# Linear attention: two of four q products inside the layer norm, weighting by pairs of tiles, and a projection that begins per tile

## The reference

```python
Q = relu(proj(Wq, bq)); K = relu(proj(Wk, bk)); V = proj(Wv, bv)
decay = exp(-pos / n)[None, None, :, None]
Q = Q * decay
K = K * decay
KV = einsum('bhnd,bhne->bhde', K, V)
Ksum = K.sum(axis=2)
Z = 1.0 / (einsum('bhnd,bhd->bhn', Q, Ksum)[..., None] + EPS)
out = einsum('bhnd,bhde->bhne', Q, KV) * Z
return einsum('bnm,dm->bnd', out, Wo) + bo
```

## Time and profile before

| | |
|---|---|
| runs | 2073.14, 2076.76, 2078.67 us (median 2076.76) |
| profiled execution, its own time | 2071.96 us |
| its span, first to last instruction | 2069.9 us |
| busy: TensorE / VectorE / ScalarE / GpSimd | 88% / 54% / 37% / 27% of the span |
| mean granted TensorE clock | 0.928 |

### The profile page before, as it was taken

One profiled execution on the slowest core, in us unless ns is written; L12 is line 12 of the kernel. 1 busy time (PEld: TensorE's weight loads), 2 busy tenths in 40 slices (PEclk: granted clock), 3 DMA queues, 4 the chain that ended last, 5 costly groups with the idle time before them and its releaser, 6 DMA issues.

```text
span 2069.9 us, 32796 instructions
## 1 busy us (share of the span) xinstructions
PE 1826.2 (88%) x10672; PEld 1016.8 (49%) x10673; DVE 1124.2 (54%) x2329; ACT 757.5 (37%) x1469; POOL 554.8 (27%) x950
## 2 busy tenths in 40 slices
PE   7799999998789996868999697899777999988895
PEld 4344444443456664565666456565443444355553
DVE  6688888884422224762222447532356888665323
ACT  3277777776311111121111112122033667731210
POOL 2322222221211112531111311464032222224630
PEclk9699999998789997978999799999886999999998
DMA  3311111123300003010000221123123112011241
GB/s 108 91 32 39 38 37 40 41 54 151 124 18 25 20 25 99 1 43 18 25 20 25 91 92 43 52 86 124 41 63 72 30 31 40 2 44 61 84 135 41
DMA packets 82064, 114.22 MB, mean 55 GB/s; under 512 B 17273, under 2 KB 61465, under 8 KB 81177
## 3 DMA queue, kind: packets, MB, share of 16 engines
q1 hardware_dynamic: 70808, 82.23, 14.0%
q0 software_dynamic: 11136, 30.42, 4.6%
HBM read 78.35 MB, written 33.69 MB: 54 GB/s over the span
## 4 chain that ended last, share of the span: by engine, by line
PE 70%; DVE 18%; issue 4%; DMA 3%; POOL 1%; ACT 1%; SPq 0%; POOLq 0%; DVEq 0%; ACTq 0%
PE psum L1521 13%; PE psum L1051 8%; PE psum L1035 7%; DVE region_a L799 7%; PE psum L1542 6%; PE psum L996 6%; PE psum L1757 5%; PE psum L1731 3%; PE psum L1775 2%; DVE x_res L1427 2%; PE psum L1776 2%; PE psum L1531 2%; PE psum L1742 2%; DVE ln_stats L269 1%; PE psum L925 1%
## 5 line engine op out<-in xcount | busy, mean ns | idle before, releaser
L799 DVE TENSOR_REDUCE region_a<-psum 128x1 f32<-128x640 f32 (+7 forms) x576 | 528.2, 954 | 108.7 <-PE psum L1001 57.5
L903 ACT ACTIVATE region_w<-psum 128x512 f32<-128x512 f32 x864 | 465.6, 600 | 221.3 <-PE psum L1035 217.8
L1521 PE MATMUL psum<-region_w,region_a 128*128 x608 | 271.1, 599 | 1.5 <-DVE region_a L1602 1.2
L1051 PE MATMUL psum<-region_w,region_a 128*32 128x512 f32 (+3 forms) x2304 | 254.1, 515 | 1.0 <-POOL region_w L726 0.6
L726 POOL TENSOR_SCALAR_AFFINE_SELECT region_w<-region_w 128x512 f32<-128x512 f32 x192 | 122.3, 637 | 457.1 <-ACT region_w L903 452.9
L996 PE MATMUL psum<-region_a,y_norm 48*128 48x512 bf16 (+7 forms) x816 | 224.4, 351 | 4.9 <-DVE region_a L799 4.0
L1416 POOL DMA_INDIRECT answer_rows<-region_a x116 | 114.7, 989 | 420.1 <-ACT region_a L1571 345.6
L1035 PE MATMUL psum<-y_norm,region_a 51*128 51x512 bf16 (+1 forms) x612 | 205.5, 399 | 5.5 <-DMA y_norm<-region_a 3.7
L1521 PEld LDWEIGHTS psum<-region_w,region_a 128*128 128x128 f32 x608 | 113.9, 193 | 132.1 <-issue 132.1
L1609 DVE TENSOR_TENSOR region_a<-psum,region_a 128x512 f32<-128x512 f32 x76 | 52.6, 692 | 215.1 <-PE psum L1521 215.1
L1412 POOL DMA_INDIRECT region_a<-token_rows,region_a x116 | 113.1, 975 | 146.6 <-DVE region_a L1388 86.8
(11 more groups left out here) (218 smaller groups left out, 2636.3 us busy)
## 6 DMA issues: line engine op xcount, KB each, us to landing
y_norm<-a_q SPq DMA_DIRECT2D x132, 64.0 KB
token_rows<-y_norm SPq DMA_DIRECT2D x16, 512.0 KB, 5.2
y_norm<-answer_rows SPq DMA_DIRECT2D x16, 512.0 KB, 6.3
y_norm<-b_q SPq DMA_DIRECT2D x36, 128.0 KB
region_w<-in_f_wg SPq DMA_DIRECT2D x1, 4096.0 KB, 13.4
region_w<-in_f_wu SPq DMA_DIRECT2D x1, 4096.0 KB, 13.5
region_w<-in_f_wd SPq DMA_DIRECT2D x1, 4096.0 KB, 14.9
region_w<-answer_rows SPq DMA_DIRECT2D x8, 512.0 KB, 8.4
```

The costliest lines, as they stand in the source:

```text
L799: dve.tensor_reduce(dst, src, AX_X, ALU.max, negate=True).then_inc(self.ring_done.sem, 1)
L903: act.activation(self.p[col % P_RING][:, :, i % 4, :], c.bank[ST_BANKS[s % 3]].rearrange("p (h t) -> p h t", h=GQ), ACT.Exp, scale=self.sc ...
L1051: mm = pe.matmul(c.bank[ACC_BANK][32 * h:32 * h + 32, P * lo:512], self.vp[slot][:, j, :], self.p[col % P_RING][:, h, lo:4, :], start=(j = ...
L1521: mm = pe.matmul(bank[:, :], self.yt[:, f, :], w[:, f, bass.ds(own * self.hidden + 512 * half, 512)], start=(f == 0), stop=(f == FT - 1))
```

## The change

1. `LayerNorm` gets hooks. Ahead of the transposes of group 2, TensorE does the q product of group 0, and ahead of those of group 3 that of group 1; ScalarE does the two relus behind its copies of groups 1 and 2. `LinearAttention.tensor` does the q products of groups 2 and 3 alone. The routing's own early products go through the same hook at the place that they had.
2. The weighting goes by pairs. With the decay cancelled, the denominator is the product of undecayed q plus `EPS / decay`, a table computed once by two small operations. A pair takes one addition, one reciprocal and two weightings in place of eight operations.
3. The projection's transposes of group 0 wait for the four tiles of that group; the wait for all 16 tiles goes ahead of the first product that writes banks 0 to 3.

```diff
 class LayerNorm(Stage):
     def turn(self, pe, g):
-        if g == 3 and self.early_logits:
-            self.ready(pe, 1)
-            self.early_logits(pe, 0)
-            self.early_logits(pe, 1)
+        if self.early:
+            self.early.before_turn(pe, g)
...
     def scalar(self, act):
...
+            if self.early:
+                self.early.behind_copies(act, g)
...
 class Project(Stage):
...
         def multiply(g):
             copied(0, g)
             copied(1, g)
+            if g == 0:
+                self.products_free(pe)
...
 class LinearAttention(Stage):
...
+    def before_turn(self, pe, g):
+        if g >= 2:
+            self.multiply_q(pe, g - 2)
+
+    def behind_copies(self, act, g):
+        if g in (1, 2):
+            self.relu_q(act, g - 1)
+
+    def multiply_q(self, pe, g):
+        c = self.c
+        if g == 0:
+            pe.wait_ge(self.w_in, self.W_IN)
+        self.ln.ready(pe, g)
+        for o in range(FT):
+            if g:
+                pe.wait_ge(self.q_done, FT * (g - 1) + o + 1)
+            for f in range(FT):
+                mm = pe.matmul(c.bank[o][:, :], self.wq[:, f, P * o:P * o + P], c.yt[:, f, 512 * g:512 * g + 512],
+                               start=(f == 0), stop=(f == FT - 1))
+            mm.then_inc(self.qprod, 1)
...
     def tensor(self, pe):
...
-        pe.wait_ge(self.w_in, self.W_IN)
         for g in range(NG):
-            self.ln.ready(pe, g)
-            for o in range(FT):
...
+            if g >= 2:
+                self.multiply_q(pe, g)
...
     def vector(self, dve):
         dve.wait_ge(self.w_in, self.W_IN)
+        dve.reciprocal(self.eps, self.decay).then_inc(self.den_step, 1)
+        dve.wait_ge(self.den_step, 1)
+        dve.tensor_scalar(self.eps, self.eps, self.EPS, None, ALU.mult).then_inc(self.den_step, 1)
...
-        for t in range(NT):
-            z = c.bank[t % 4][:, 0:FT * (P + nh)].rearrange("p (f e) -> p f e", f=FT)
-            den, rden = self.den[t % 2], self.rden[t % 2]
-            decay = self.decay[:, t % BT:t % BT + 1]
-            dve.wait_ge(self.outp, t + 1)
-            dve.tensor_scalar(den, z[:, :, P:P + nh], decay, self.EPS, ALU.mult, ALU.add).then_inc(self.den_step, 1)
-            dve.wait_ge(self.den_step, 3 * t + 1)
+        for n in range(NT // 2):
+            den, rden = self.den[n % 2], self.rden[n % 2]
+            both = c.psum[:, 2 * (n % 2):2 * (n % 2) + 2, 0:FT * (P + nh)].rearrange("p n (f e) -> p n f e", f=FT)
+            eps = over(self.eps[:, 2 * n % BT:2 * n % BT + 2], 2, FT * nh)
+            dve.wait_ge(self.outp, 2 * n + 2)
+            if n == 0:
+                dve.wait_ge(self.den_step, 2)
+            dve.tensor_tensor(den.rearrange("p n (f h) -> p n f h", f=FT), both[:, :, :, P:P + nh],
+                              eps.rearrange("p n (f h) -> p n f h", f=FT), ALU.add).then_inc(self.den_step, 1)
+            dve.wait_ge(self.den_step, 2 * n + 3)
             dve.reciprocal(rden, den).then_inc(self.den_step, 1)
-            dve.wait_ge(self.den_step, 3 * t + 2)
-            dve.tensor_scalar(den, rden, decay, None, ALU.mult).then_inc(self.den_step, 1)
-            dve.wait_ge(self.den_step, 3 * t + 3)
-            dve.tensor_tensor(c.cx[:, D * t:D * t + D].rearrange("p (f h e) -> p f h e", f=FT, h=nh),
...
+            dve.wait_ge(self.den_step, 2 * n + 4)
+            for i in range(2):
+                t = 2 * n + i
+                dve.tensor_tensor(c.cx[:, D * t:D * t + D].rearrange("p (f h e) -> p f h e", f=FT, h=nh),
...
     def finished(self, pe, g):
-        pe.wait_ge(self.o_done, 4 * g + 4 if g else NT)
+        pe.wait_ge(self.o_done, 4 * g + 4)
+
+    def products_free(self, pe):
+        pe.wait_ge(self.o_done, NT)
```

More of the change, by code:

```diff
@@ L176, in tile_done, with before_turn, behind_copies, products_free @@
     def tile_done(self, dve, t): pass
+    def before_turn(self, pe, g): pass
+    def behind_copies(self, act, g): pass
+    def products_free(self, pe): pass
     def sync(self, sp): pass
@@ L247, in __init__ @@
         before.next_norm = self
-        self.early_logits = None
+        self.early = None
     def ready(self, eng, g):
@@ L332, in scalar, with __init__ @@
                                ACT.Copy).then_inc(done, 1)
+            if self.early:
+                self.early.behind_copies(act, g)
 class Project(Stage):
     turns_next_norm = True
-    def __init__(self, c, k, source, w, before):
-        self.c, self.k, self.source, self.w, self.before = c, k, source, w, before
+    def __init__(self, c, k, mixer, w):
+        self.c, self.k, self.source, self.w, self.before = c, k, mixer.source, w, mixer.finished
+        self.products_free = mixer.products_free
         self.turned = c.shared_sem("project_turned")
@@ L1167, in __init__ @@
         all_steps = (13 if top == 2 else 6) + 5 + (e - 1) + 5 * top + 2 + 2 + (4 if top == 2 else 0)
-        ln.early_logits = self.multiply_logits
+        ln.early = self
         (self.w_in, self.const_in, self.prod, self.logits_set, self.step, self.shifted, self.exp, self.orders, self.hits, self.before,
@@ L1212, in gpsimd @@
                 pool.memset(spare[:, :, j:j + 1], float(P * j)).then_inc(self.orders.sem, 1)
+    def before_turn(self, pe, g):
+        if g == 3:
+            self.ln.ready(pe, 1)
+            self.multiply_logits(pe, 0)
+            self.multiply_logits(pe, 1)
     def multiply_logits(self, pe, g):
@@ L2091, in __init__ @@
         self.bd = [r.take([FT, P + self.nh]) for _ in range(NB)]
-        self.den = [r.take([FT, self.nh]) for _ in range(2)]
-        self.rden = [r.take([FT, self.nh]) for _ in range(2)]
+        self.den = [r.take([2, FT * self.nh]) for _ in range(2)]
+        self.rden = [r.take([2, FT * self.nh]) for _ in range(2)]
+        self.eps = r.take([BT])
         self.k = r.take([NT, D])
+        ln.early = self
         r = Carve(c.region["w"], at)
@@ L2120, in gpsimd, with before_turn, relu_q @@
             pool.tensor_tensor(c.x[:, t, :], c.x[:, t, :], self.bo, ALU.add).then_inc(self.biased, 1)
+    def before_turn(self, pe, g):
+        if g >= 2:
[15 more added lines that the diff above has]
+            mm.then_inc(self.qprod, 1)
+    def relu_q(self, act, g):
+        c = self.c
+        if g == 0:
+            act.wait_ge(self.w_in, self.W_IN)
+        for o in range(FT):
+            act.wait_ge(self.qprod, FT * g + o + 1)
+            act.activation(self.qt[:, o, 512 * g:512 * g + 512], c.bank[o][:, :], ACT.Relu,
+                           bias=self.bq[:, o:o + 1]).then_inc(self.q_done, 1)
     def tensor(self, pe):
         c, nh = self.c, self.nh
-        pe.wait_ge(self.w_in, self.W_IN)
         for g in range(NG):
-            self.ln.ready(pe, g)
-            for o in range(FT):
[L2128 to L2133, removed]
+            if g >= 2:
+                self.multiply_q(pe, g)
             for t in range(4 * g, 4 * g + 4):
@@ L2161, in scalar @@
     def scalar(self, act):
[L2162 to L2168, removed]
+        for g in range(2, NG):
+            self.relu_q(act, g)
     def vector(self, dve):
@@ L2191, in vector @@
                                   ALU.mult).then_inc(self.bd_done, 1)
[L2192 to L2205 removed]
+        for n in range(NT // 2):
[8 more added lines that the diff above has]
+            dve.wait_ge(self.den_step, 2 * n + 3)
+            dve.reciprocal(rden, den).then_inc(self.den_step, 1)
+            dve.wait_ge(self.den_step, 2 * n + 4)
+            for i in range(2):
+                t = 2 * n + i
+                dve.tensor_tensor(c.cx[:, D * t:D * t + D].rearrange("p (f h e) -> p f h e", f=FT, h=nh),
+                                  both[:, i, :, 0:P].rearrange("p f (h e) -> p f h e", h=nh),
+                                  over(rden[:, i, :].rearrange("p (f h) -> p f h", f=FT), 3, self.HEAD),
+                                  ALU.mult).then_inc(self.o_done, 1)
         dve.wait_ge(self.biased, NT)
@@ L2333, in project @@
         def project(name, mixer, w):
-            p = Project(c, counts["project"], mixer.source, w, mixer.finished)
+            p = Project(c, counts["project"], mixer, w)
             counts["project"] += 1
```

## The result

The changed kernel takes **2056.22 us** (median of 4 runs, 2052.26 to 2059.95); the kernel before, run beside it, 2075.44 (4 runs, 2073.14 to 2078.67). The ratio is 0.9902, with a 95% interval of 0.9882 to 0.9921: about 20 us faster, between 16 and 25 (the two medians lie 19.2 apart). The forecast was 2058.5, and 18.2 us less. The profiled execution of the changed kernel took 2058.68 us, its span is 2056.6.

The account below looks back on a forecast made before the run. VectorE paced layer norm and weighting, TensorE q, k and v. Gains 6.6 + 7.6 + 4.0 = 18.2 us, taken from the 2071.96 us profiled execution, gave 2053.8, and 2058.5 us against the 2076.76 median; range 2052 to 2066.

Parts of the forecast that it names:

- q: Layer norm: q of groups 0 and 1 moved there starts the sums over tokens 7.0 us sooner; gain 6.6 us.
- 0.4 for the clock: Start of early q: a later clock rise loses between 0 and 0.8 us; 0.4 us was taken off the gain.
- The first q: Layer norm, from 1179.2 us: q of group 0 costs 5.44 us because its clock has to rise, against 3.43 otherwise.
- the clash of GpSimd with the k tiles: k and v tiles: bias additions lengthen one VectorE operation to 1.00 us, still under TensorE's 1.72 per tile; cost nothing.
- The other covers: Layer norm: ScalarE's relus hide behind q, VectorE's last copy moves to about 1190 us, loads have 1.4 us to spare.
- Pairs: Weighting: 1.33 us per pair, eight pairs 10.6 us against 18.6 us; gain 7.6 us after 0.4 for the first pair.
- The wait for the second tile of the first pair: Start of the weighting: the first pair waits for its second tile at most 0.53 us; 0.4 us taken.
- Per tile: Projection: last weighting to second projected tile takes 3.1 us instead of 7.1, with TensorE at 2.4 GHz; gain 4.0 us.
- The clock at the projection: Rival: the clock falls at the projection, costing 2.6 us; gain 15.6 us, 2061.2 us in all; chance 0.08.
- A late clock: Rival: early q in the layer norm does not raise the clock until the old time; gain 14.4, 2062.4 us; chance 0.07.
- turns without overlap: Rival: in the weighting TensorE and VectorE take turns, 2.63 us per pair; gain 8.2, 2068.6 us; chance 0.04.
- a clock that stays low: Rival: TensorE stays at 1.2 GHz past the layer norm; some 39 us slower, 2116 us; chance 0.02.

Follow-up runs that it names:

- clearing later: The changed kernel, with GpSimd's clearing of the next block's weight buffer waiting until all 16 k tiles are done: 2055.36 us, ratio 0.9917, stage 77.04 us.
- q alone: The kernel before plus only the q products of groups 0 and 1 inside the layer norm: 2067.56 us, ratio 0.9945, stage 88.07 us.
- pairs alone: The kernel before plus only the weighting by pairs: 2067.72 us, ratio 0.9959, stage 87.59 us; run again unchanged, 2064.83 us, stage 87.61 us.
- without per tile: The changed kernel with the projection's transposes waiting for all 16 tiles again: 2054.05 us, ratio 0.9889, stage 78.85 us.

## Why the prediction was right

The three gains came where they were placed, 7.38, 8.06 and 3.94 for 6.6, 7.6 and 4.0; the stage saved 19.38 us for 18.2. The total lies 2.3 us under the forecast, within the spread of the runs; 1.3 of it is the median of before, which a fourth run moved from 2076.76 to 2075.44. That the medians differ by 19.2 us, so close to the stage, is luck in part: the two profiled spans differ by 13.3, since the rest of the program wanders by several us.

*q.* From the end of group 1's transposes the forecast had 45.1 and 0.4 for the clock, 45.5; the chain has 44.73 (1180.35 to 1225.08). The first q took 4.82 where 5.44 and the 0.4 stood, a gain of 1.02: the clock rose 3.8 us after the work began to flow (from the last transposes ahead of q, 1179.23 to 1183.0). The forecast's 4.3 was counted from about 1187.7; counted alike, from the transposes at 1186.99 that run straight into q, it is 5.0 before. So the clock rose sooner than in either row that the forecast had (5.0, and 5.7 at the projection). The transposes took 0.87 each, not 0.95, which is 0.16. Against that stands the one step that failed: "I cost it at nothing", for the clash of GpSimd with the k tiles. It cost 0.38, as clearing later shows. The prediction read the row as a clash with GpSimd's bias additions, but the earlier trace rows is a relu beside the clearing, and it met it half-way, 1.00 us; one that meets the clearing's start lasts until 0.15 behind the clearing's end. The bias additions alone stretch a relu to 0.83 at most, which costs nothing. The Trainium skill has a rule that bears on this (SBUF — State Buffer, Who interferes with whom): a VectorE operation in one of its two-port modes, which `tensor_scalar` can enter, and GpSimd exclude each other from a shared pair of ports; whoever issues first has it for a whole instruction, and the other blocks. The ends of the relus, 0.15 behind the clearing both times, agree with that; whether the relu was in such a mode no run shows, and by the starts in the rows of after the relu began 0.12 before the clearing and was yet the one that waited. The other covers held: ScalarE's relus, the later copy of the last half group (1190.39, forecast about 1190), and the loads, with some 2.5 us to spare for a forecast 1.4.

*Pairs.* 1.27 us for a forecast 1.33: the reciprocal of 32 took 0.35 as estimated, the addition 0.18 instead of at least 0.22, and 0.21 to the next operation instead of 0.26. Here the price by the page was the nearer one: by the Trainium skill (VectorE: DVE Perf Modes, the errata section) 158 ns, an estimate, against 0.18 measured. The wait for the second tile of the first pair was 0.23 (8.51 less 8.28), not 0.4. One row was misread without harm: the 0.63 us per tile of the earlier trace rows are the idle time of TensorE's weight loads; its matmuls idled for 0.45, and the sum uses neither.

*Per tile.* The size was right, 3.94, and the transposes ran at the fast clock, as the row of the layer norm had them and against the rule on transposes named there. The reason was only partly right. The forecast counted the pause and the low clock of before as both removed by the new waits. Without them the stage is 1.4 us longer, not 3.9: with q and the pairs in place the pause is 1.62 instead of 3.84, and the clock holds. So the 4.0 is what the new waits are worth by themselves (3.92 measured), not what they add to the other two parts; the sum is right because the low stretch was counted once.

*The rivals.* The clock at the projection: not here, but q alone and pairs alone show the fall (transposes of 3.42 and 3.48 us), so it was near. A late clock, turns without overlap, and a clock that stays low: none was seen; 1.00 from 1183.0 to 1288.

## What to carry to other kernels

Measure each part from a mark of its own stage, not from the start of the program: here a stage repeats to 0.12 us, where the whole wanders by 7.7 (2052.26 to 2059.95 for the changed kernel). Where several edits touch one stall, cost the stall once, and say which edit removes it when the others are already there. For a clash of VectorE with a long write of GpSimd take the worst meeting of the two, the whole of the long instruction, not the one overlap that the trace of before happens to show.

## What the runs showed of the hardware

The clock's low stretch ahead of the layer norm began 3.0 to 3.3 us before its first statistics in every run, though that start wandered over 6.6 us, and the falls inside the stage repeat to 0.05 us relative to it (88.92 twice, 82.11 and 82.15); in the last block they don't, even between two profiles of the kernel before. An equal pause of 1.62 us ahead of the projection's transposes came with a fall of the clock in one kernel (pairs alone) and not in another (without per tile). Transposes alone, in the layer norm's pauses, raised the clock to 1.00 for 3.4 us but did not hold it; matmuls in the same pauses did. A VectorE operation of 0.35 us beside a GpSimd write of 1.80 us took up to 2.20 us.
